# A graph layer on one core: k rows of three groups of edges, not of one, made from gathered x rows; a ring of eight groups; an edge operand split in halves

## The reference

```python
h = jnp.maximum(_layernorm(x, axis=-1), 0.0)         # x: (6250, 256)
eq = h @ Wq + bq
ek = h @ Wk + bk
e = edge_attr_256 @ We + be                          # (106250, 256)
m = jax.nn.relu(eq[dst] + ek[src] + e)
ft = jax.ops.segment_sum(m, dst, num_segments=6250)
out = x + (ft @ Wr + br)
```

## Time and profile before

| | |
|---|---|
| three runs | 1126.44, 1127.38, 1129.05 us, median 1127.38 |
| profiled execution | 1127.15 us, span 1125.3 us, granted clock 0.998 |
| busy share | PE 96%, DVE 85%, ACT 76%, POOL 75% |
| chain that ended last | POOL 72%, issue 24% |
| data | 308.88 MB, mean 274 GB/s; POOL's gathers 109 MB of it |

### The profile page before, as it was taken

One profiled execution on the slowest core, in us unless ns is written; L12 is line 12 of the kernel. 1 busy time (PEld: TensorE's weight loads), 2 busy tenths in 40 slices (PEclk: granted clock), 3 DMA queues, 4 the chain that ended last, 5 costly groups with the idle time before them and its releaser, 6 DMA issues.

```text
span 1125.3 us, 28375 instructions
## 1 busy us (share of the span) xinstructions
PE 1085.7 (96%) x9170; PEld 1063.5 (95%) x9170; DVE 952.0 (85%) x1425; ACT 855.8 (76%) x1373; POOL 843.3 (75%) x947
## 2 busy tenths in 40 slices
PE   8989999999999999999999999999999999999997
PEld 8989999999999999999999999999999999998997
DVE  7878888888888888888888888888888888887886
ACT  7968877777777777777777778777787777876774
POOL 8877777777777777777777777777777777777773
PEclk9999999999999999999999999999999999999999
DMA  9889999999999999999999899999898998998882
GB/s 299 267 241 304 288 281 275 286 276 288 278 282 285 278 285 278 280 282 276 287 277 280 284 272 288 274 283 285 271 290 274 285 287 273 288 278 268 265 252 86
DMA packets 170744, 308.88 MB, mean 274 GB/s; under 512 B 30568, under 2 KB 116981, under 8 KB 170661
## 3 DMA queue, kind: packets, MB, share of 16 engines
q1 hardware_dynamic: 130212, 198.57, 53.4%
q0 software_dynamic: 39888, 108.97, 35.8%
q10 hardware_dynamic: 560, 0.52, 0.1%
HBM read 280.99 MB, written 26.95 MB: 274 GB/s over the span
## 4 chain that ended last, share of the span: by engine, by line
POOL 72%; issue 24%; PE 1%; DVE 1%; ACT 1%; DMA 1%; POOLq 0%; ACTq 0%; DVEq 0%; SPq 0%
POOL k_rows L714 69%; POOL hn L641 1%; PE p_sum L1360 0%; POOL window_cols L592 0%; DMA src_idx<-in_src_lanes 0%; POOL edge L654 0%; PE p_edge L1360 0%; ACT k_rows L784 0%; ACT hn L757 0%; PE p_sum L1476 0%; DVE stats L1002 0%; PE p_turn L1380 0%; DVE m_lo L1193 0%; DMA k_rows<-k_table,idx 0%; POOL norm L619 0%
## 5 line engine op out<-in xcount | busy, mean ns | idle before, releaser
L714 POOL DMA_INDIRECT k_rows<-k_table,src_idx x796 | 764.1, 960 | 242.8 <-issue 242.8
L1360 PE MATMUL p_edge<-we_hi,edge_hi 128*128 128x256 f32 x1662 | 471.7, 284 | 28.6 <-DVE m_lo L1193 27.3
L1360 PE MATMUL p_edge<-we_hi,edge_lo 128*128 128x256 f32 x1662 | 461.3, 278 | 0.0
L1360 PE MATMUL p_edge<-we_lo,edge_hi 128*128 128x256 f32 x1662 | 460.0, 277 | 0.0
L1184 DVE TENSOR_TENSOR p_edge<-p_edge,k_rows 128x1024 f32<-128x1024 f32 x208 | 256.1, 1231 | 153.5 <-DMA k_rows<-k_table,src_idx 112.8
L866 ACT ACTIVATE m_hi<-p_edge 128x1024 fp32r<-128x1024 f32 x208 | 213.8, 1028 | 204.6 <-DVE p_edge L1184 204.6
L1360 PEld LDWEIGHTS p_edge<-we_hi,edge_hi 128*128 128x128 f32 x1662 | 313.4, 189 | 46.6 <-ACT pick L858 21.4
L1360 PEld LDWEIGHTS p_edge<-we_lo,edge_hi 128*128 128x128 f32 x1662 | 314.3, 189 | 0.0
L1360 PEld LDWEIGHTS p_edge<-we_hi,edge_lo 128*128 128x128 f32 x1662 | 312.1, 188 | 0.0
L1159 DVE TENSOR_TENSOR edge_lo<-edge,edge_hi 128x1024 fp32r<-128x1024 f32 x208 | 253.5, 1219 | 0.0
L1193 DVE SCALAR_TENSOR_TENSOR m_lo<-p_edge,m_hi 128x1024 fp32r<-128x1024 f32 x208 | 253.3, 1218 | 0.0
(11 more groups left out here) (159 smaller groups left out, 1111.2 us busy)
## 6 DMA issues: line engine op xcount, KB each, us to landing
edge<-in_edges SPq DMA_DIRECT2D x208, 512.0 KB, 5.2
rel_row<-rel_table SPq DMA_DIRECT2D x208, 96.0 KB
q_win<-q_table SPq DMA_DIRECT2D x416, 48.0 KB
k_rows<-k_table,src_idx POOLq DMA_INDIRECT x796
q_table<-hn SPq DMA_DIRECT2D x46, 256.0 KB
pre<-in_x SPq DMA_DIRECT2D x55, 128.0 KB, 3.7
out_rows<-pre SPq DMA_DIRECT2D x55, 128.0 KB, 1.7
k_table<-k_rows SPq DMA_DIRECT2D x23, 256.0 KB, 3.5
```

The lines of the kernel that those rows point to most:

```text
L714: nc.gpsimd.indirect_dma_start(out=k_rows[:, slot, j, :], out_offset=None, in_=k_table, in_offset=bass.IndirectOffsetOnAxis(ap=offsets, ax ...
L1360: ins = nc.tensor.matmul(target, a(h), b[:, h, :], start=(start and h == 0 and n == 0), stop=(stop and h == HALVES - 1 and n == 2))
```

## The change

Three groups take their k rows from gathered x rows: six edge pairs instead of two, twelve x gathers instead of four. POOL makes the means of all of them at once, and centres the first two; VectorE centres the other four and pairs 20 to 22, which POOL did before. A small load of the first source numbers, issued by ScalarE, comes ahead, and the first x gathers stand ahead of POOL's first `mean`. The ring `k_rows` has eight groups (gather of n waits for the add of n-8), for which `window_cols` and `rel_idx` give up memory. `edge_low` is made in two halves, one ahead of `message_low` and one behind it; `edge_product` now waits for both in every group. The extra rows lie in the last two places of the ring until they are centred.

```diff
+X_GROUPS = 3
+X_TILES = X_GROUPS * TILES
+EARLY_TILES = 3
+EDGE_PAIRS = X_TILES // 2
-VECTOR_PAIRS = range(14, 20)
+VECTOR_PAIRS = range(14, 23)
+POOL_EDGE_PAIRS = NODE_PAIRS + 2
+X_STATS_OF_PAIR = {18: 4, 19: 1, 20: 3, 21: 3, 22: 1}
+KRING = 2 * UNROLL
...
-            nc.gpsimd.iota(window_cols[:], pattern=[[1, PASSES * WIN]], base=0, channel_multiplier=0,
+            nc.gpsimd.iota(window_cols[:], pattern=[[1, WIN]], base=0, channel_multiplier=0,
+                           allow_small_or_imprecise_dtypes=True).then_inc(s_later, 1)
+            nc.gpsimd.iota(pass_start[:], pattern=[[WIN, PASSES]], base=0, channel_multiplier=0,
                            allow_small_or_imprecise_dtypes=True).then_inc(s_later, 1)
...
+            later_constants()
+            pool.wait_ge(s_first, 16)
+            gather_x(range(EARLY_TILES))
             for part in range(3):
+                if part == 2:
+                    gather_x(range(EARLY_TILES, TILES))
                 mean(part)
...
                 if i == 14:
                     variance(4)
-                    gather_x(range(1))
+                    gather_x(range(TILES, TILES + 1))
                     mean(5)
                     variance(5)
                 if i == 15:
                     refine(4)
-                    gather_x(range(1, 3))
+                    gather_x(range(TILES + 1, X_TILES - 1))
                 if i == 16:
-                    later_constants()
-                if i == 17:
-                    gather_x(range(3, TILES))
-                if i == 21:
                     refine(5)
+                    gather_x(range(X_TILES - 1, X_TILES))
...
-                after(pool, s_pre, n - 4)
+                after(pool, s_pre, n - KRING)
...
             act.dma_start(w_raw[:, :, 0:D], Wk.rearrange("(h p) n -> p h n", p=LANES)).then_inc(s_wk, 16)
+            act.dma_start(src_idx[:, 0:X_GROUPS, :], src_lanes[:, 0:X_GROUPS, :]).then_inc(s_first, 16)
...
+                for k in range(x_stats_done(i), x_stats_done(i + 1)):
+                    row_statistics(k)
...
-                    edge_low(it, u + 2)
+                    edge_low(it, u + 2, 0)
                     message_low(it, u)
+                    edge_low(it, u + 2, 1)
...
-            for i in range(NODE_PAIRS, ALL_PAIRS):
+            for i in range(NODE_PAIRS, NODE_PAIRS + 2):
                 turn_h(i)
             for i in range(NODE_PAIRS, ALL_PAIRS):
                 k_product(i)
+                if i + 2 < ALL_PAIRS:
+                    turn_h(i + 2)
             turn_ident(WARM_LAST, p_turn)
...
-                if isinstance(n, int) and n < 2:
-                    after(pe, s_elo, n)
+                after(pe, s_elo, HALVES * n + HALVES - 1)
```

More of the change, by code:

```diff
@@ L500, in _ @@
             store_first_q(1)
+            sp.wait_ge(s_blo, 2)
+            for n, part in enumerate((bq_hi, bq_lo)):
+                sp.dma_start(q_win[2 * WIN + n:2 * WIN + n + 1, :, :].bitcast(F32),
+                             part[:].bitcast(F32).unsqueeze(1).to_broadcast([1, UNROLL, D])).then_inc(s_bqrow, 16)
             sp.wait_ge(s_qfirst[0], 16 * 2)
@@ L505, in _ @@
             load_window(0, 2)
+            after(sp, s_hT, NODE_PAIRS + TILES // 2 - 1)
             load_edge(0, 3)
@@ L508, in _ @@
             load_window(0, 3)
+            after(sp, s_hT, ALL_PAIRS - 1)
+            load_next_x(0)
             def load_tail_x():
@@ L694, in _ @@
             variance(NODE_PARTS)
-            for i in range(NODE_PAIRS + 1, ALL_PAIRS):
+            for i in range(NODE_PAIRS + 1, POOL_EDGE_PAIRS):
                 pool_centre(i)
@@ L714, in gather @@
                     nc.gpsimd.indirect_dma_start(
[L715 removed]
+                        out=k_rows[:, place, j, :], out_offset=None, in_=k_table,
                         in_offset=bass.IndirectOffsetOnAxis(ap=offsets, axis=0),
                         engine_sem=s_wrote,
[L718 to L723 removed]
+                    ).then_inc(s_rows[place], 16)
+            for u in range(X_GROUPS, UNROLL):
+                gather(0, u)
+            pairs = pairs_of_passes(pool)
+            for u in range(UNROLL):
+                if u == 1:
                     pool.wait_ge(s_esplit, 2)
                     pool.wait_ge(s_rsplit, 2)
[L726 to L728 removed]
+                if u > 1:
+                    after(pool, s_hn0, NODE_PAIRS + 2 * u - 1)
+                    after(pool, s_hn1, NODE_PAIRS + 2 * u - 1)
+                gather(1, u)
+            for it in range(2, K_STATIC):
                 for u in range(UNROLL):
                     gather(it, u)
[L731 to L733 removed]
+            with pool.Fori(K_STATIC // 2, pairs - 1) as pair:
+                for half in range(2):
+                    for u in range(UNROLL):
+                        gather((pair, half), u)
             for u in range(UNROLL):
[L735 removed]
+                gather((pairs - 1, 0), u)
+            for u in range(UNROLL):
+                gather((pairs - 1, 1), u, LAST_TILES if u == UNROLL - 1 else TILES)
         @block.scalar
@@ L838, in _ @@
             copy_k(NODE_PAIRS - 1)
-            for i in range(NODE_PAIRS + 1, ALL_PAIRS):
-                centre(i, 1)
+            centre(NODE_PAIRS + 1, 1)
             deviation(NODE_PARTS)
@@ L1006, in stats_done, with x_stats_done @@
                 return STATS_AHEAD + sum(STATS_OF_PAIR[:i])
+            def x_stats_done(i):
+                return NODE_BLOCKS + sum(n for at_pair, n in X_STATS_OF_PAIR.items() if at_pair < i)
             def inverse(part):
@@ L1298, in _ @@
             dve.wait_ge(s_prep, PREP_STEPS + 1)
-            bodies = passes_of(dve)
+            pairs = pairs_of_passes(dve)
             steps(0, first=True, q=True)
-            for it in range(1, STATIC_BODIES):
+            for it in range(1, K_STATIC):
                 steps(it, q=it < Q_BODIES)
-            with dve.Fori(STATIC_BODIES, bodies - 1) as it:
-                steps(it)
+            dve.wait_ge(s_cleared, CLEAR_BODIES + 1)
+            with dve.Fori(K_STATIC // 2, pairs - 1) as pair:
+                steps((pair, 0))
+                steps((pair, 1))
+            steps((pairs - 1, 0))
+            bodies = pairs * 2
             def tail_low(t):
@@ L1319, in last_steps @@
                         after(dve, s_fhi, it)
-                    add_rows(it, u, True)
+                    add_rows((pairs - 1, 1), u, True)
                     make_send(it, u)
@@ L1328, in last_steps @@
                 w0 = window_of(it, 0)
-                add_rows(it, 3, True)
+                add_rows((pairs - 1, 1), 3, True)
                 after(dve, s_flo, it)
```

213 lines of the change are left out of this document (112 added, 101 removed).

## The result

| | before | after |
|---|---|---|
| median (runs) | 1128.66 us (5) | 1152.25 us (5), from 1151.95 to 1153.14 |
| ratio | | 1.0214, 95% interval 1.0199 to 1.0229 |
| profiled execution | 1127.15, span 1125.3 | 1153.14, span 1151.3 |

What follows compares the result with a forecast made beforehand. POOL's gathers were taken to bound the kernel. Against the profiled 1127.15 us, -10.0 + 2.5 + 2.6 + 9 + 6 = +10.1 gave 1137 us; the 8-in-10 range was 1121 to 1146, the forecast's own 1130 to 1146.

Steps and rivals of the forecast that it cites:

- Removed gathers: POOL's k-row gathers: groups 1 and 2 no longer gather, eight gathers fewer at 0.95 + 0.30 us, -10.0 us.
- POOL's start: Kernel start: x gathers waiting for a small load delay POOL's first mean from 7.37 to 9.9, +2.5 us; bounds 0 and 3.3.
- The end of the k phase: Turn of pair 23: late mean of the extra rows and late eighth x gather, +2.6 us for the two, bounds 0 to 5.
- the bound of 5: Upper bound for the k phase's end, if TensorE idles some 3 us and then gets half a clock.
- The time in which POOL is ahead: Early groups: gathers meet VectorE's instructions at random for 52 groups, losing 14 against 5.3 us before; +9, bounds +2 and +14.
- The collision rule: A gather starting during VectorE's edge_low takes longer by what is left less 0.13 us; a started gather isn't disturbed.
- The time in which POOL paces: Later bodies: edge_low's second half delays the fourth gather, 0.2 us a body over some 38 bodies, +6; bounds 0 and +12.
- The third rival: Consumers become the bound: a body needs 20 us also with POOL ahead, nothing is caught up; +11, 1138 us; chance 0.08.
- my short start: Delay of the first add, edge_product(0, 0): 5.1 from start and k phase plus 6 for extra pairs, from 77.6 to 88.7.
- The first: Rival that POOL's early lead is kept: blocked time less than 5 us more over the run, 1122 us; chance 0.22.
- what would show it: Trace signs: mean 9.9, pair 23 4 to 5 later, k gather 69 to 71, add 87 to 90, gathers over 1.0 to 340.
- sign of being wrong: First k gather before 67, gathers' mean before the meeting under 0.98, or POOL seen waiting for pre.

Runs made afterwards that it cites:

- e7: Changed kernel with the first x gathers ahead of POOL's third mean and the extra rows' mean behind the centring of pair 24; 1.0202 times before.
- e11: Changed kernel with edge_low in one piece, the old distance of 97344 bytes and two places of POOL's start program undone; 1.0076 times before.
- e10: Changed kernel with edge_low in one piece again, ahead of message_low, on a chip with the full clock; 1.0105 times before.
- e8: Changed kernel with stats moved ahead of the weights and unused bytes in its place, so edge_hi lies 97344 bytes behind we_hi as before; 1.017 times before.
- e16: Kernel before with only edge_low in two halves, one ahead of message_low and one behind, on a full-clock chip; 1.0062 times before.
- e12: Changed kernel with POOL's gather of group n waiting for the add of n-4, the eight ring places kept; 1.025 times before.
- e14: e11 with the last x gather ahead of refine of the last node part and not behind it; 1.0075 times before.
- m2: Separate kernel, TensorE alone: bursts of 48 matmuls with the loaded operand moved in steps of 32 bytes; the spacing repeats after 256 bytes.
- m1: Separate kernel of 48-matmul bursts with operands at places of before, after, mixed and shifted; before's took 117.7 then 113.3 ns, after's 117.9 and 117.7.
- e15: Kernel before with edge_low in two halves, one ahead of message_low and one behind, on a slow chip; 1.0011 times before.
- e1: Changed kernel with an unused 32-byte tile ahead of w_hi, shifting all large tiles, on a slow chip; 1.0329 times before.
- e4: Kernel before with only edge_low in two halves as in the change, on a slow chip; 1.0101 times before.

## Why the prediction was wrong

**Removed gathers, -10.0.** Right.

**POOL's start, +2.5: direction right, size +3.6.** The first x gather started at 6.82, where I had put the load at 5.9; it took 1.62 and the other two 0.95 each, together about what I had counted.

**The end of the k phase, +2.6: +5.8.** Both reasons held (the mean behind the last statistics, the late landing), and they add up where I had them side by side: the landing came late for the statistics (58.84), these held up `h_low` of pair 22 (59.83), and only behind that stood the last statistic and the mean. The gather itself was only 0.9 later than worked out, once the 3.6 of the start are taken off (54.08 - 3.6 against 49.6). Pair 23 was turned 7.75 later, 4.15 without the start; the other 1.6 came between that turn and the first k gather, where the half clock that I had kept for the bound of 5 came. e7 shows that the two places account for 3.9 of the 9.4 at the first gather.

**The time in which POOL is ahead, +9: +17.4. This is the step that failed**, and within it the line "POOL then needs 5.28 a group and VectorE 4.78 to 4.9 (the halves add 0.07, and TensorE now waits for the second half)". POOL needed 1.033 + 0.30 = 1.333 a gather, 5.33 a group. The consumers needed 20.09 / 4 = 5.02. The gap of some 23 us closed by 0.31 a group and not by 0.45: some 75 groups and not 52. And each group cost POOL more: 0.34 over 947 ns a gather, up to 460 us, where I had 0.27. This loss was 24.4 and not 14 (over 954 ns, as in the sum above, 22.4); of the 10 us between, the number of groups and the loss a group make about half each. Two things made the 5.02; with both undone (e11) it is 19.33 / 4 = 4.83, inside my 4.78 to 4.9. The wait for the second half, which I had named and priced at under 0.1 a group, costs 0.40 to 0.61 us a body, 0.10 to 0.15 a group (20.09 against 19.69 in e10; 19.94 against 19.33, e8 against e11). And the spacing of matmuls, which no part of my reading could show, costs 0.36 with `edge_low` in one piece (19.69 against 19.33) and 0.15 with halves (20.09 against 19.94). My base was one single body of 19.1. The collision rule itself held: of 243 gathers from 125 to 450 us, 65 started during an `edge_low`, each was longer by what was left of it less 0.13 (by nothing where less was left), within 0.01, and they hold 20.6 of the 21.4 us by which all are over 0.947. What failed is that they meet at random. As many met as chance gives, but at their start 0.44 us of a half were left on average, where a random meeting leaves 0.34; why isn't known.

**The time in which POOL paces, +6: +8.3.** The mechanism is right: the second half from 610.72 to 611.40 catches the gather that starts at 611.17, which takes 1.05 and not 0.95 (0.23 left less 0.13):

```profile
610.72 0.68 DVE L1201 TENSOR_TENSOR edge_lo<-edge,edge_hi 128x512 fp32r<-128x512 f32 x1
611.17 1.05 POOL L746 DMA_INDIRECT k_rows<-k_table,src_idx  x1 [0.30 <-issue]
```

From 480 to 860 the excess over 0.947 is 0.33 us a body and was 0.10, +0.22 where I had put 0.2. The body rose by more, 0.27; e16 puts the halves alone at 0.17 a body, 7 us over the run, and e8 the slower matmuls at 0.1.

**Rivals.** The third rival's mechanism (a body of 20 us also when POOL is ahead) is what happened for 18 bodies, though POOL was caught up all the same, slowly; I had set it against the earlier trace rows and given it 0.08. Its time, 1138, was too low since it took over my short start (the first add came 16.1 us later and not 11.1) and counted nothing behind the meeting. The first fell: it allowed under 5 us more of blocked time over the run, and there were 25.7 (17.4 + 8.3). e11 leaves +8.6 us with no halves and the old distance: start +8.7, gathers -10.0, and those with POOL ahead longer by about 11 (38 of 1055 ns and 163 of 1028 in place of 44 of 1068). That the three groups can't pay here is thus shown for this arrangement only. Of "what would show it", the first `mean` (9.9), the turn of pair 23 (4 to 5 later), the first k gather (69 to 71) and the first add (87 to 90) were each missed on the high side. The gathers' means were as said, over 1.0 while POOL was ahead, but up to some 475 us and not 340, and 0.967 to 0.970 behind that. No sign of being wrong that I had named came.

## What to carry to other kernels

A lead of the engine that paces is worth less than it looks: while it runs ahead it meets its neighbour's instructions at any point of their group, and much of the lead is paid back (some 10 of 14 us in e12; in e14 about half of 3.4). Before an operand is made later, even by half, look at who waits for it when the pacing engine is ahead, not only when it paces; here the place of half an operand cost 12 us of 24. And after a change that resizes tiles, compare the spacing of matmuls that follow each other without a wait, before explaining anything by instructions.

## What the hardware showed unexpectedly

The spacing of 128x256 matmuls in fp32r, each with its own loaded operand, depends on the distance in SBUF between the operand that is loaded and the one that streams, in m2 with a period of 256 bytes: 117.4 to 119.8 ns with all other engines idle, and in m1 a second mode of 113.3 to 113.8 at a distance of 64. Something else acts too, up to 1.3 ns at one distance. 384 bytes more between two tiles made the matmuls of a real kernel's edge product 3.5% slower; undoing it in the changed kernel gave back 0.4% of its time. The Trainium skill (TensorE: Matmul & The Clock Gate, section "Back-to-back issue gap") gives N / 2.4 + 2.5 ns for isolated matmuls, 109.2 at N = 256, and says that in a stream of weight loads and matmuls both set the spacing. The bursts here are such a stream; their lowest mean was 113.3, and only at one distance. The Trainium skill (SBUF — State Buffer, section "Who interferes with whom") gives TensorE two independent read ports, for the moving operand and for the weights. The bursts of m2 differ in nothing but the address of the loaded operand, and their spacing differs by 2.4 ns. That the two reads disturb each other is the likely reading; no run here looks at the ports themselves.

Chips differ more than kernels: the kernel before took 1128 to 1129 us on four of six chips, and 1511 and 1569 on the two others, where the granted clock was 0.88 to 0.92 in place of 1.00. The clock alone doesn't explain that. Timeline of e15, TensorE in the middle of a stream of matmuls, and two stretches:

```profile
236.78 0.29 PE L1479 MATMUL p_sum<-m_lo,send 128*48 128x256 f32 x1 [0.83 <-issue]
236.91 0.28 PE L1479 MATMUL p_sum<-m_hi,send 128*48 128x256 f32 x1
238.18 0.37 PE L1479 MATMUL p_sum<-m_lo,send 128*48 128x256 f32 x1 [0.99 <-issue]
...
231.00:235.00 4.00, 4.00 (x37) 4.00 (x36) 2.79 (x7) 2.59 (x5) 3.08 (x4) 1.00 0.89 306
...
238.00:242.00 4.00, 3.19 (x15) 3.04 (x15) 1.38 (x2) 1.75 (x4) 0.33 (x1) 0.50 0.27 84
```

TensorE stands still, waits for nothing that the profile shows, and only then is granted 0.50 (1.2 GHz). The traces of e1 to e4 and e15 each have over 300 such places with more than 0.5 us between two starts, some 290 us in all; those of the kernel before and the changed one, on chips with the full clock, have one and two. What makes the pauses isn't known, nor, as each chip was met once, whether they belong to the chip or to the time of the run.
